# Q and output projections of a two-layer cross-attention kernel: channel chunks of 128, 128 and 64, the third with high and low parts in one chunk, the bias as two rows beside ones

## The reference, cut to what matters

```
q   = x @ Wq                                  # 320 -> 320 channels
... keys and values from text and image rows, softmax per head,
... a second softmax over image rows, with a similarity term
hs  = text_out + ip_out                       # [256, 320]
out = hs @ Wout + bout + x                    # 320 -> 320 channels, bias, residual
```

## Time and profile before

| what | value |
|---|---|
| runs | 1708.06, 1701.98, 1714.18 us |
| profiled execution | 1715.15 us, its span 1713.0 us |
| mean granted TensorE clock | 0.988 |
| TensorE matmuls | 1625.4 us busy, 95% of the span |
| VectorE | 1380.9 us, 81% |
| ScalarE | 1033.4 us, 60% |
| GpSimd | 833.2 us, 49% |
| chain of waits that ended last | TensorE 78%, VectorE 9%, ScalarE 4% |

### The profile page before, as it was taken

The page is one execution under the profiler, slowest core; times in us unless marked ns, Lnnn a source line. Parts: engine busy times, 40 slices in busy tenths (PEclk is TensorE's granted clock), DMA queues, the critical chain, the costliest instruction groups (busy, mean ns, idle before and its releaser), DMA issues.

```text
span 1713.0 us, 42882 instructions
## 1 busy us (share of the span) xinstructions
PE 1625.4 (95%) x14568; PEld 1440.6 (84%) x14568; DVE 1380.9 (81%) x3630; ACT 1033.4 (60%) x2204; POOL 833.2 (49%) x691
## 2 busy tenths in 40 slices
PE   4899999999999999999999999999999999999986
PEld 4788888888888888877888888898889888898965
DVE  4577777777777777866889988999889999999884
ACT  3366665666665666655666666666666666666652
POOL 4422222222222222333577667766677566756663
PEclk9999999999999999998999999999999999999998
DMA  7433343334333433543233323332333223332211
GB/s 204 99 105 109 116 122 112 120 117 122 115 116 114 121 113 117 152 118 90 82 96 100 99 65 87 104 97 81 85 98 103 80 72 97 108 87 55 83 29 41
DMA packets 185985, 172.72 MB, mean 101 GB/s; under 512 B 25760, under 2 KB 185770, under 8 KB 185770
## 3 DMA queue, kind: packets, MB, share of 16 engines
q1 hardware_dynamic: 185770, 169.98, 34.1%
HBM read 110.17 MB, written 57.76 MB: 98 GB/s over the span
## 4 chain that ended last, share of the span: by engine, by line
PE 78%; DVE 9%; ACT 4%; issue 4%; POOL 2%; SPq 2%; DMA 1%; DVEq 0%; ACTq 0%; POOLq 0%
PE MISC L101 25%; PE GP L101 16%; PE NAT L226 9%; PE TR L256 7%; PE PV L303 4%; PE PV L287 4%; PE PV L284 2%; PE PV L306 2%; PE MISC L335 2%; DVE PM L819 2%; DVE TA L806 1%; PE MISC L476 1%; ACT PVS L541 1%; PE PV L244 1%; ACT PH L534 1%
## 5 line engine op out<-in xcount | busy, mean ns | idle before, releaser
L970 POOL TENSOR_TENSOR ZS<-ZP 128x256 f32<-128x256 f32 x267 | 267.2, 1001 | 230.7 <-DVE ZP L813 230.6
L527 ACT ACTIVATE P<-TA 128x512 f32<-128x512 f32 x320 | 202.0, 631 | 269.4 <-DVE TA L806 269.0
L226 PE MATMUL NAT<-KS,QS 65*128 65x256 f32 x1280 | 295.6, 313 | 9.5 <-DMA KS<-qk_parts 5.7
L256 PE MATMUL TR<-QS,KS 69*128 69x256 f32 (+1 forms) x1280 | 272.0, 294 | 0.3 <-DVE TA L806 0.2
L975 POOL TENSOR_TENSOR PARTS<-QKF,PARTS 112x512 fp32r<-112x512 f32 (+3 forms) x96 | 126.7, 1320 | 293.6 <-ACT PARTS L555 293.6
L226 PEld LDWEIGHTS NAT<-KS,QS 65*128 65x128 f32 x1280 | 203.0, 191 | 73.5 <-issue 63.5
L101 PE MATMUL GP<-PH,GH 128*128 128x256 f32 (+1 forms) x960 | 244.2, 285 | 15.9 <-DVE ZP L813 15.9
L813 DVE TENSOR_TENSOR ZP<-GP,PM 128x512 f32<-128x512 f32 x320 | 219.2, 685 | 46.5 <-PE GP L101 43.8
L819 DVE SCALAR_TENSOR_TENSOR PM<-P,PH 128x512 f32<-128x512 f32 x320 | 252.3, 788 | 0.0
L797 DVE TENSOR_REDUCE MX<-NAT 128x2 f32<-128x504 f32 x320 | 216.0, 675 | 33.2 <-PE NAT L226 30.4
L101 PE MATMUL GP<-PH,GL 128*128 128x256 f32 (+1 forms) x960 | 240.9, 279 | 0.0
(11 more groups left out here) (279 smaller groups left out, 3959.9 us busy)
## 6 DMA issues: line engine op xcount, KB each, us to landing
QS<-qk_parts SPq DMA_DIRECT2D x480, 64.0 KB
KS<-qk_parts SPq DMA_DIRECT2D x480, 64.0 KB
qk_parts<-PARTS SPq DMA_DIRECT2D x128, 224.0 KB, 2.8
CT<-in_ctx_t SPq DMA_DIRECT2D x32, 512.0 KB, 4.2
qk_parts<-PARTS SPq DMA_DIRECT2D x64, 192.0 KB, 2.4
QS<-NH SPq DMA_DIRECT2D x480, 4.0 KB
XT<-in_x_t SPq DMA_DIRECT2D x48, 112.0 KB, 2.2
XT<-x_t SPq DMA_DIRECT2D x48, 112.0 KB, 2.3
```

Source lines behind the costliest of these rows:

```text
L226: ins = e.matmul(NAT[s % 2][:, i * T:(i + 1) * T], QS[0:KQ, h, i * 128:(i + 1) * 128], KS[0:KQ, h, :], start=True, stop=True)
L256: ins = e.matmul(TR[s % 2][:, i * S:(i + 1) * S], KS[0:w, h, i * 128:(i + 1) * 128], QS[0:w, h, :], start=True, stop=True)
L527: e.activation(P[:, s % NP, :], TA[:, s % 2, :], ACT.Exp, scale=SCALE).then_inc(q["exp"], 1)
L970: e.tensor_tensor(ZS[s % NZ][:, :], ZP[:, s % 2, 0:S], ZP[:, s % 2, S:2 * S], ALU.add).then_inc(q["zs"], 1)
```

## The change

- New chunks: rows 0 to 127, 128 to 255, and the last 64 channels (TAIL). XTS becomes one tile of five chunks: 0 and 1 are high parts; chunk 2 has the tail's low part in rows 0 to 63 and its high part in rows 64 to 127; chunks 3 and 4 are the low parts of 0 and 1. The last 64 rows of x and of the weights are loaded twice, into both halves of chunk 2.
- `product8` makes 8 matmuls where `product3` made 9. The last pair of the Q product contracts over the 64 rows at partitions 64 to 127. The last pair of the output product uses a new tile HT2 (the tail's high part in rows 0 to 63, ones in rows 64 and 96, zeros between) over 97 rows; the bias's high and low parts stand in rows 64 and 96 of the low weight.
- HS and VIP become 384 wide, their last 64 channels twice. ScalarE copies those of HS (`dup`, slot 47 of a batch in layer 0, 70 in layer 1), VIP is loaded by two DMAs and masked by two operations. The transposes have 128 weight columns instead of 112.
- Each half of HT now has two ScalarE copies (HT, HT2) and two VectorE subtractions (256 and 128 elements a row, where one had 384), and twice the increments are waited for.
- `load_x` and the weight loads issue four DMAs instead of three. The bias goes by two DMAs into spare rows of NH. SyncE waits, ahead of the first of them, for VectorE to have cleared those rows (`bias` >= 1), and VectorE makes the two weight rows at slot NORM+3 and, for layer 1, at WO_LO+1. The clears of the overlapping weight rows go.

```diff
+TAIL = C - 256
+BH, BL = TAIL, TAIL + 32
...
+def product8(e, out, x, w, x2, w2, flip):
+
+    pairs = [(x[0], w[0][0]), (x[1], w[0][1]), (x[2], w[0][2]), (x[3], w[0][0]), (x[4], w[0][1]), (x[0], w[1][0]), (x[1], w[1][1]), (x2, w2)]
+    return product(e, out, [(b, a) if flip else (a, b) for a, b in pairs])
...
-                    product3(e, k[:, 0:C], HT, WO, lambda x, c: x[0:CK, c, i * 128:(i + 1) * 128],
-                             lambda w, c: w[0:CK, c, :], 3).then_inc(q["om"], 1)
+                    product8(e, k[:, 0:C], [HT[:, c, own] for c in range(5)], [[w[:, c, :] for c in range(3)] for w in WO],
+                             HT2[:, own], WO[1][0:BL + 1, 2, :], False).then_inc(q["om"], 1)
...
-                    product3(e, k[0:mn, 0:S], WQ, XTS, lambda w, c: w[0:CK, c, m0:m0 + mn], lambda x, c: x[0:CK, c, :], 3)
+                    product8(e, k[0:mn, 0:S], [XTS[:, c, :] for c in range(5)], [[w[:, c, m0:m0 + mn] for c in range(3)] for w in WQ],
+                             XTS[TAIL:128, 2, :], WQ[1][TAIL:128, 2, m0:m0 + mn], True)
...
     @block.scalar
+            for b in both(t, AT0["dup"], AT1["dup"]):
+                e.wait_ge(*((q["hs"], b + 1) if b < B else (q["tx"], b - B + 1)))
+                e.copy(HS[:, :, C:384], HS[:, :, 256:C]).then_inc(q["dup"], 1)
...
-                    e.copy(HT[0][0:CK, :, i * 128:(i + 1) * 128],
-                           ring.bank["hst", b, i][0:CK, 0:384].rearrange("p (c q) -> p c q", c=3)).then_inc(q["ht_hi"], 1)
+                    k = ring.bank["hst", b, i]
+                    e.copy(HT[:, 0:3, i * 128:(i + 1) * 128], k[:, 0:384].rearrange("p (c q) -> p c q", c=3)).then_inc(q["ht_hi"], 1)
+                    e.copy(HT2[0:TAIL, i * 128:(i + 1) * 128], k[0:TAIL, 256:384]).then_inc(q["ht_hi"], 1)
...
     @block.vector
-        e.memset(WQR[1][0:TWICE, 2, :], 0.0).then_inc(q["clear"], 1)
-        e.memset(WOR[1][0:TWICE_O, 2, :], 0.0).then_inc(q["clear"], 1)
+        def bias_rows(n):
+            e.wait_ge(q["w_b"], 32 * n + 32)
+            e.tensor_copy(WO[1][BH:BL + 1, 2, :], BR[BH:BL + 1, :]).then_inc(q["bias"], 1)
+            e.wait_ge(q["bias"], 2 * n + 2)
+            e.tensor_tensor(WO[1][BL:BL + 1, 2, :], BR[BL:BL + 1, :], WO[1][BL:BL + 1, 2, :].bitcast(F32), ALU.subtract).then_inc(q["bias"], 1)
...
-        e.memset(HS[:, :, C:C + 1], 1.0).then_inc(q["fill"], 1)
         e.memset(ONES, 1.0).then_inc(q["fill"], 1)
+        e.memset(HT2[BH:BL + 1, :].bitcast(F32), 0.0).then_inc(q["ones2"], 1)
+        e.memset(BR[BH:BL + 1, :], 0.0).then_inc(q["bias"], 1)
...
-                    e.wait_ge(q["ht_hi"], 2 * b + i + 1)
-                    e.tensor_tensor(HT[1][0:CK, :, i * 128:(i + 1) * 128],
-                                    ring.bank["hst", b, i][0:CK, 0:384].rearrange("p (c q) -> p c q", c=3),
-                                    HT[0][0:CK, :, i * 128:(i + 1) * 128].bitcast(F32), ALU.subtract).then_inc(q["ht_lo"], 1)
+                    e.wait_ge(q["ht_hi"], 4 * b + 2 * i + 2)
+                    k, own = ring.bank["hst", b, i], slice(i * 128, (i + 1) * 128)
+                    e.tensor_tensor(HT[:, 3:5, own], k[:, 0:256].rearrange("p (c q) -> p c q", c=2), HT[:, 0:2, own].bitcast(F32),
+                                    ALU.subtract).then_inc(q["ht_lo"], 1)
+                    e.tensor_tensor(HT[0:TAIL, 2, own], k[0:TAIL, 256:384], HT[0:TAIL, 2, own].bitcast(F32),
+                                    ALU.subtract).then_inc(q["ht_lo"], 1)
...
     @block.sync
-            for c, c0 in enumerate(CC):
-                e.dma_start(dst[TWICE * (c // 2):CK, c, :], w[c0 + TWICE * (c // 2):c0 + CK, :]).then_inc(sem, 16)
+            for c, r0, n in ((0, 0, 128), (1, 0, 128), (2, 0, TAIL), (2, TAIL, TAIL)):
+                e.dma_start(dst[r0:r0 + n, c, :], w[128 * c:128 * c + n, :]).then_inc(sem, 16)
...
-        load_out(WOR[1], a["L0_xattn_Wout"], a["bias0"], q["w_o"])
+        load_rows(WOR[1], a["L0_xattn_Wout"], q["w_o"])
+        e.wait_ge(q["bias"], 1)
+        load_bias(a["bias0"])
```

More of the change, by code:

```diff
@@ L351, in _ @@
                         e.wait_ge(q["hs"], b + 1)
-                    for c, c0 in enumerate(CO):
-                        ins = e.transpose(k[0:CK, c * 128:(c + 1) * 128], HS[:, i, c0:c0 + CK], IDENT[:, :])
+                        e.wait_ge(q["dup"], b + 1)
+                    for c in range(3):
+                        ins = e.transpose(k[:, c * 128:(c + 1) * 128], HS[:, i, 128 * c:128 * c + 128], IDENT[:, :])
                     ins.then_inc(q["hst"], 1)
@@ L361, in _ @@
                         e.wait_ge(q["tx"], b + 1)
+                        e.wait_ge(q["dup"], B + b + 1)
                         e.wait_ge(q["pt"], b + 1)
-                        e.wait_ge(q["vip"], b + 1)
-                    for c, c0 in enumerate(CO):
-                        e.matmul(k[0:CK, c * 128:(c + 1) * 128], HS[:, i, c0:c0 + CK], IDENT[:, :], start=True, stop=False)
-                        ins = e.matmul(k[0:CK, c * 128:(c + 1) * 128], VIP[:, b % 2, c0:c0 + CK], PT[:, i * 128:(i + 1) * 128], start=False, stop=True)
+                        e.wait_ge(q["vip"], 2 * b + 2)
+                    for c in range(3):
+                        e.matmul(k[:, c * 128:(c + 1) * 128], HS[:, i, 128 * c:128 * c + 128], IDENT[:, :], start=True, stop=False)
+                        ins = e.matmul(k[:, c * 128:(c + 1) * 128], VIP[:, b % 2, 128 * c:128 * c + 128], PT[:, i * 128:(i + 1) * 128], start=False, stop=True)
                     ins.then_inc(q["hst"], 1)
@@ L944, in _ @@
                     e.memset(VB[96:N2, p, 1, :, D:D + 1], 1.0).then_inc(q["vfix"], 1)
+            if t == NORM + 3:
+                e.wait_ge(q["ones2"], 1)
+                e.memset(HT2[BH:BH + 1, :].bitcast(F32), 1.0).then_inc(q["ones2"], 1)
+                e.memset(HT2[BL:BL + 1, :].bitcast(F32), 1.0).then_inc(q["ones2"], 1)
+                e.wait_ge(q["w_lo"], 4)
+                bias_rows(0)
+            if t == WO_LO + 1:
+                e.wait_ge(q["w1_lo"], 4)
+                bias_rows(1)
             if t == S1 - LEAD + 1:
@@ L1013, in _ @@
             if b is not None:
[L1014 to L1015 removed]
+                e.wait_ge(q["vip_in"], 32 * (b + 1))
+                for c0, c1, f0 in ((0, C, 0), (C, 384, 256)):
+                    e.tensor_tensor(VIP[:, b % 2, c0:c1], VIP[:, b % 2, c0:c1], VMASK[:, f0:C], ALU.mult).then_inc(q["vip"], 1)
             if t == NORM:
```

118 lines of the change are left out of this document (56 added, 62 removed).

## The result

The changed kernel took 1753.07 us (median of 4 runs, 1751.43 to 1754.5) where the kernel before, on the same chip, took 1711.12. The ratio is 1.0237, 95% interval 1.0205 to 1.0268. That is outside the predicted range, and twice the predicted loss: 40.5 us by the ratio (42 by the two medians) instead of 21.

The account below looks back on a forecast made before the run. TensorE was taken as the bound, busy over 98% of the steady part. TensorE's net 10.7, HT 4.2, dup 1.0, layer 1 1.3, bias 0.5 and start 3 made +20.7 us on 1708.1: 1729 us, range 1696 to 1744.

Parts of the forecast that it names:

- the 64-row matmul: Q product's last matmul: changing array shape costs 0.34 us a visit, 96 visits, +32.6 us, nine tenths of TensorE's net counted.
- the start: Before the first batches: SyncE's wait for VectorE's clear, ten DMAs behind it, an added x DMA and bias rows; +3 us.
- the Q product's matmuls saved: Q products on TensorE: one matmul in nine goes, 96 x 0.1175 = 11.3 us saved, nine tenths of TensorE's net counted.
- the output part: Output projection: 64 matmuls of 0.147 us go, 9.4 us saved, against added copies, subtractions, duplicate and bias work.
- bias steps: Two steps where VectorE makes bias rows, held about 1.4 us, delaying its maxima; +0.5 us for layer 1's, nothing to 3.
- Layer 1. [...] +1.3 us: Layer 1: TensorE's 13 waits for the bank that HTL frees each grow by 0.07 to 0.1 us; +1.3 us.
- Rival A: Q product's last matmul: 64 rows run at the same 0.12 us pace, no shape change; 1699 us, chance 0.23.
- B: Whole kernel: as Rival A, and new copies, duplicate and SyncE's wait cost nothing; 1687 us, chance 0.05.
- Rival C: Q product's last matmul: each visit costs 0.45 us; 1740 us, up to 1745 with VectorE fuller in layer 1; chance 0.10.
- the bound of 7: At the start: the prediction is wrong if the start has moved by more than 7 us.
- Waits behind the HT halves: Layer 0: longer copies and subtractions delay VectorE's maxima, so TensorE waits; 0.26 us a batch, 16 batches, +4.2 us.
- The dup: Layer 0: ScalarE's copy of HS lands where TensorE wants the transposes; 0.06 us a batch, +1.0 us, at most 4.3.

Follow-up runs that it names:

- full_height: Changed kernel with the Q product's last matmul contracting over all 128 rows of chunk 2 instead of 64; ratio 1.0038 to the kernel before.
- before_64_rows: Kernel before with only the ninth matmul of each Q product cut from 112 rows to 64; ratio 1.0190 to the kernel before.
- the Q part alone: Kernel before with the new x and Wq layout, eight full-height matmuls a Q product, and the old output part; ratio 0.9932 to the kernel before.
- f1=70: Changed kernel, full-height last Q matmul, VectorE's bias clear first, layer 1's FU pair at step 70 for 71; ratio 0.9966 to the kernel before.
- dup46_no_third_copies: early_clear_dup46 without VectorE's 64x128 HT subtractions and ScalarE's HT2 copies, result incomplete, for timing only; ratio 0.9901 to the kernel before.
- early_clear_dup46: Changed kernel, full-height last Q matmul, VectorE's bias clear first, layer 0's HS duplicate at step 46 behind SN, ST; ratio 0.9985 to the kernel before.

## Why the prediction was wrong

By the ratios, with 1% as 17 us:

| term | predicted, us | measured, us |
|---|---|---|
| the 64-row matmul | +29 | +34 (after and full_height), +33 (before_64_rows) |
| the start | +3 | +9.8 and +8.6 |
| the Q product's matmuls saved | -10 | -12 |
| the output part: matmuls saved, HT halves, dup, layer 1, bias steps | -1.5 | +8 |

The step that failed by most is the output part, and in it the term "Layer 1. [...] +1.3 us": the part was to win a little and cost 8 us. In layer 0 the batch grew by 0.11 us against the Q part alone, about 2 us in all; the rest lies in layer 1, where the batches of the profiled executions went from 55.7 to 56.3 us on average. The start is second, off by 6 to 7 us, and the shape third.

**The shape of the 64-row matmul: right, and counted a little low.** I took 0.34 us a visit from the group of 64 weight columns; it is 0.36 in layer 0 and 0.33 to 0.37 in layer 1. The parts were much as described, too, 0.09 ahead and 0.10 on the NAT pair, and 0.18 between where I had 0.14. Taking nine tenths of it was wrong: per layer-0 batch all of it shows. 96 x 0.36 = 35 us, where I had 32.6 x 0.9 = 29. Rival A, no change of shape, and with it B, are refuted by before_64_rows. Rival C named 0.45 a visit, which it was not; the total only passed C's for the reasons below.

**"The start. [...] +3 us": right in kind, mis-sized.** The wait and the ten DMAs behind it were right, and so, nearly, was the first spill: 33.41 us where I had 32 (36.66 in full_height). The error was in the sentence that gave the stacks and the first NAT only 2 us: the wait cost the first NAT 5.4 us in one pair of kernels and 9.5 in the other, the second with a VectorE copy of 3.07 us ahead of the clear. The ratios with and without the wait give 9.8 and 8.6 us, beyond the bound of 7 that I had named as a sign of being wrong, though their intervals reach below it.

**"Layer 1. [...] +1.3 us": its mechanism was missed, and it is the largest miss.** The bank that HT frees was waited for 13 times, 4.5 us in all, little over the earlier trace rows. What I did not see is that layer-1 batches have a long state, which the earlier trace rows could not show: in the kernel before four of twelve were long, in the kernel after all. Who waited for whom in the kernel after:

```profile
PE MISC L352 <- DVE GL L781: 13.7, 13, 1.1
```

In the kernel before, the same wait was there four times. Per batch the output part saves 0.29 us in layer 1 and the batch grows by 56.13 - 55.55 = 0.58 against the short batches of the Q part alone. f1=70 takes 0.58 back, and leaves the batch at 55.59, no shorter than without the part. Of the 0.3 us that it should have saved, 0.2 are the chain of copies: with the chain cut (dup46_no_third_copies) two of the twelve batches were short at 55.38 and 55.39 and the others long at 55.95 to 56.16, where early_clear_dup46 has 55.6 and 56.1, and TensorE's waits for the bank that HT frees fell from 4.3 us to 2.0 over them. The last 0.1 us stays open. Why nearly all batches are long with the output part and only one to four of twelve without it was not found either.

**"Waits behind the HT halves": right in kind, too small.** I had 0.26 us a batch against the kernel before; it is 44.83 - 44.43 = 0.40, and 0.47 for the two small operations alone. The wait I named, before line 335's transposes, stayed at 0.7 us. The one that counts is the bank of the V product. In the kernel before it already started 0.05 us after HTL's end at 577.68:

```profile
577.73 0.37 PE L101 MATMUL GP<-WVH,CTSH 128*77 128x320 f32 x1
```

I had looked only at VectorE's lateness, and not at who takes the bank next.

**The dup: nearly nothing,** as taken; moving it changed the batch by 0.02 us.

**The removed matmuls.** In the Q part they count in full (0.37 and 0.35 us a batch for 0.35; 12 us in total for 11.3, with an interval of 8 to 16). In the output part the 9.4 us are eaten by the part's own costs: in layer 0 0.40 us a batch of bank, 6 us, and in layer 1 the long batches, 0.58 x 16 = 9 us at most, with the chain of copies on top.

The measured terms of the table add up to the 40.5 us of the total because each is the difference of two neighbouring kernels on one path from before to after; that sum is no further proof. What supports the terms is the second measurement where there is one (height, start) and the batches.

## What to carry to other kernels

Keep the contraction of a lone matmul above 64 rows when its neighbours are taller: here rows that add a harmless term cost nothing (65, 112 and 128 rows kept the pace), and going to 64 and back cost 0.36 us. Before merging work into fewer matmuls, list who takes each PSUM bank next, since one small added operation before the bank comes free can cost more than the matmul saved. A wait put into a DMA queue also takes over the spread of what it waits for: a copy of 0.13 us in one execution and 3.07 in another moved the first NAT by 3.3 us. Before explaining where a stretch grew, compare it with the kernel that has the cause removed, and look at its granted clock.

## What the hardware showed unexpectedly

- The step is sharp: 65 rows run at 0.12 us, 64 rows cost 0.36 us more per visit, whichever half of the partitions they use.
- A layer of identical batches can sit in one of two lengths, 55.55 and 56.1 us, and what tells them apart is one VectorE operation that meets a row of GpSimd operations: 0.68 us becomes 2.35.
- Where the two layers meet, three batches took between 142 and 151 us in nearly the same schedule, and the batch in question 52.4 us at a mean granted clock of 1.00 and 61.0 at 0.83. No experiment here was aimed at what lowers the clock there, and it is the main reason why single spans mislead by more than the effects at stake.
